# A decoder kernel whose key-mask products take 64 rows in place of six

## The chip, the cores and the metric

The kernel runs on one core of a Trainium2 chip. Its time is the device time of one execution in microseconds, taken as the median over several executions.

## What is computed

Two decoder layers on x (16 sequences of 64 tokens, 128 features), each with self attention, cross attention to a context of 64 tokens, and a feed-forward part; a layer norm follows every residual sum. Layer 0 has rotary causal self attention and a mixture of eight experts of which each token takes two; layer 1 has wide self attention (16 heads of 64) and a ternary feed-forward part. Both cross attentions are narrow (16 heads of 8 features) and have a key mask:

```python
q, k, v = split_heads(x @ Wq.T), split_heads(ctx @ Wk.T), split_heads(ctx @ Wv.T)
scores = einsum('bhqd,bhkd->bhqk', q, k) / sqrt(8)
scores = where(mask == 0, NEG, scores)      # NEG: -1e9 in layer 0, -1e12 in layer 1
out = einsum('bhqk,bhkd->bhqd', softmax(scores), v)
x = layernorm(x + out @ Wo.T)
```

(Layer 0 also has biases.) The mask is 16 x 1 x 1 x 64: one row of keys for each sequence.

## The kernel before

**Tiles.** A tile is two sequences, 128 tokens in the 128 partitions; there are eight. The program has three streams of work in order: `pre` (self0, the rotary self attention, then cross0, eight tiles each), the routed experts, and `post` (the wide self attention, then cross1, then the ternary part). self0, cross0 and cross1 are objects of one class, `Narrow`.

**Order.** Each engine runs its own loop over slots j (`stream_pe`, `stream_act`, `stream_dve`, `stream_pool`), written by hand. In slot j TensorE scores tile j-2 (`s_pe`), transposes the output of tile j-5 (`y_pe`, L582), projects queries and keys of tile j (`qk_pe`, L511) and values of tile j-2 (`v_pe`, L523), transposes the exponentials of tile j-3 (`t_pe`, L429), projects the output of tile j-5 (`o_pe`, L586), weighs the values of tile j-4 (`va_pe`, L566) and transposes a normalised tile (`x_pe`, L371). Engines are joined by semaphores; a wait stands at the start of the step that needs it.

**The scores.** For a tile, `s_pe` first makes four f32 products (L539): for each sequence b (64 query columns of the array, 64 output partitions) and each half g of the heads (64 rows of the array, one PSUM bank), queries QS against the block keys KB, 512 columns. It leaves each sum open and adds four bf16 mask products to it. In self0 (L547) the stationary operand is a 64 x 64 identity and the moving one the causal fill, 64 rows, repeated over eight heads. In the cross attentions (L550) the fill value times sqrt(8), split in three bf16 parts for each of two sequences, stands in six rows of `fills` in each half (partitions 0 to 5 and 64 to 69), and the mask of the tile's keys as 0 or 1 in the same six rows of `mrb`. The sum over the six rows adds the fill to the masked keys of the right sequence.

**What reads the scores.** The DVE takes the maximum of each head (L403) and subtracts it (L413), ScalarE makes the exponentials (L419), TensorE transposes them (L429). GpSimd (POOL) makes the block keys KB (L690), the normalisation (L331, L333, L337) and the residual with bias (L716). For a y tile the DVE makes reciprocals (L676) and ysb (L680), which `y_pe` transposes.

**The start.** POOL sets `half`, `zero` and `VB` by memsets (L1996 to L1999), waits for the constants `cst` and copies ones into `VB` (L2004). The DVE waits for the same constants, casts the identity and the causal fill to bf16 (L2031, L2032), waits for both, casts the six rows of `fills` in each half (L2035), and goes on with the first PSUM copies. TensorE waits for those fills (`s_bfc`) after its first transposes. The mask rows of `mrb` are written by the DVE in slot 2 (L1795). SP issues nearly all loads in one list, then waits for `zero` (`s_zt`), stores zeros to `routed_rows`, and loads the rest of the weights (L1945).

**The last slots of cross0** have routing work between them: in slot 16 TensorE makes the first router logits (L1364) and the DVE chooses experts from them (L1378 to L1395) before it takes the next residual; in slot 17 it turns ranks into rows (L1423 to L1430). The expert weights are transposed from L1347 on. The experts' gate products are L1549. In `post` the wide attention's last tile ends among the first tiles of cross1: L910 is its last step on POOL before the transposes of its shares.

Of the kernel before, what the change touches and what calls it, by code (L numbers as in the profile page):

```python
# [8 lines left out]
BF16 = mybir.dt.bfloat16  # L9
# [6 lines left out]
P = 128  # L16
BATCH, SEQ = 16, 64
NT = BATCH * SEQ // P
# [60 lines left out]
def decoder_kernel(nc, A, out):  # L79
    with ExitStack() as ctx:  # L80
        def sb(name, shape, dt=F32):
            return ctx.enter_context(nc.sbuf_tensor(name, shape, dt))

        def sem(name):
            return ctx.enter_context(nc.semaphore(name))
# [15 lines left out]
        def bc(ap, axis, n):  # L101

            shape = list(ap.shape)
            shape.insert(axis, n)
            return ap.unsqueeze(axis).to_broadcast(shape)
# [22 lines left out]
        bvc = sb("bvc", [P, 2])  # L128
        rowb = sb("rowb", [P, 3, P])
        mk = sb("mk", [P, NT, P])  # L130
        mrb = sb("mrb", [70, NT, SEQ], BF16)
        idb = sb("idb", [P, P], BF16)
        caus = sb("caus", [P, SEQ], BF16)
        fills = sb("fills", [70, 2, P], BF16)
        QS = sb("QS", [P, 3, P])
        TMP = sb("TMP", [P, 2, 4, SEQ])
        TC = sb("TC", [P, 2, 4, SEQ])
# [94 lines left out]
        s_mk = sem("masks_made")  # L232
        s_bf = sem("bf16_identity_made")
        s_bfc = sem("bf16_constants_made")
        s_z = sem("blocks_zeroed")
        s_tern = sem("ternary_weights_made")
        s_out = sem("output_stored")
# [214 lines left out]
        class Narrow(Stage):  # L452
# [76 lines left out]
            def s_pe(self, pe, job):  # L529
                i, n = job.i, job.n  # L530
                pe.wait_ge(*self.q_ready.at(i + 1))
                if job.before:
                    pe.wait_ge(*job.before.s_read())
                for b in range(2):
                    pe.wait_ge(*self.kb.at(2 * i + b + 1))
                    q = slice(64 * b, 64 * b + 64)
                    for g in range(2):
                        f = slice(64 * g, 64 * g + 64)
                        pe.matmul(PS[q, B_S + g, :], QS[f, n % 3, q], KB[f, n % 2, b].rearrange("p h k -> p (h k)"),  # L539
                                  start=True, stop=False)  # L540
                for b in range(2):
                    q = slice(64 * b, 64 * b + 64)
                    for g in range(2):
                        o = PS[q, B_S + g, :].rearrange("q (h k) -> q h k", h=8)
                        if self.fill is None:
                            f = slice(64 * g, 64 * g + 64)
                            m = pe.matmul(o, idb[f, f], bc(caus[f, :], 1, 8), start=False, stop=True)  # L547
                        else:
                            f = slice(64 * g, 64 * g + 6)
                            m = pe.matmul(o, fills[f, self.fill, q], bc(mrb[f, i, :], 1, 8), start=False, stop=True)  # L550
                m.then_inc(self.s_mm.sem, 1)

# [696 lines left out]
        def stream_dve(dve, tiles, extra, last):  # L1249
            for j in range(last):  # L1250
                y = at(tiles, j - 5)
                if y:
                    y.stage.y_dve(dve, y)
                t = at(tiles, j - 3)
                hidden = t and isinstance(t.stage, Ternary)
                if hidden:
                    t.stage.sum_dve(dve, t)
                ternary, others = [], []
                for x in turned(tiles, j):
                    (ternary if isinstance(x.stage, Ternary) else others).append(x)  # L1260
                for x in others:
                    x.stage.ln_dve(dve, x)
                if t and not hidden:
                    t.stage.sum_dve(dve, t)
                v = at(tiles, j - 2)
                if v:
                    v.stage.max_dve(dve, v)
                b, q = at(tiles, j), at(tiles, j - 1)
                if q:
                    q.stage.qkw_copies(dve, 1, q)  # L1270
                if v:
                    v.stage.vw_copies(dve, 1, v)
                extra(dve, j, False)
                w = at(tiles, j - 4)
                if w:
                    w.stage.ya_dve(dve, w)
                for r in summed(tiles, j):
                    r.stage.r_dve(dve, r)
                for x in ternary:
                    x.stage.ln_dve(dve, x)  # L1280
                if b:
                    b.stage.qk_dve(dve, b)
                extra(dve, j, True)

        def stream_pool(pool, tiles, extra, last):
            for j in range(last):
                t = at(tiles, j - 3)
                if t:
                    t.stage.shares_pool(pool, t)
                extra(pool, j, False)  # L1290
                b = at(tiles, j - 1)
                if b:
                    b.stage.blocks_pool(pool, b)
                b = at(tiles, j)
                if b:
                    b.stage.cos_pool(pool, b)
                if t:
                    t.stage.hidden_pool(pool, t)
                for r in summed(tiles, j):
                    r.stage.rsqrt_pool(pool, r)  # L1300
                for x in turned(tiles, j):
                    x.stage.bias_pool(pool, x)
                extra(pool, j, True)
# [574 lines left out]
        def drain_dve(dve):  # L1878
            a1.y_dve(dve, S[5])
            moe.choose(dve, 1)  # L1880
            a1.r_dve(dve, S[5])
            a1.y_dve(dve, S[6])
            a1.ln_dve(dve, S[4])
            moe.place(dve, 1)
            a1.ln_dve(dve, S[5])
            a1.r_dve(dve, S[6])
            a1.y_dve(dve, S[7])
            moe.choose(dve, 2)
            a1.ln_dve(dve, S[6])
            a1.r_dve(dve, S[7])  # L1890
            moe.place(dve, 2)
            a1.ln_dve(dve, S[7])
            moe.choose(dve, 3)
            moe.place(dve, 3)

        def drain_pool(pool):
            a1.rsqrt_pool(pool, S[5])
            moe.scatter(pool, 2, 0)
            moe.scatter(pool, 2, 1)
            a1.rsqrt_pool(pool, S[6])  # L1900
            moe.scatter(pool, 3, 0)
            moe.scatter(pool, 3, 1)
            a1.rsqrt_pool(pool, S[7])
            for t in range(4, NT):
                for r in range(2):
                    moe.scatter(pool, t, r)
# [87 lines left out]
        @block.gpsimd  # L1994
        def _(pool):
            pool.memset(half[:, :], -0.5).then_inc(s_half, 1)  # L1996

            pool.memset(zero[:, :], 0.0).then_inc(s_zt, 1)
            pool.memset(VB[:, :, :, :, :, :], 0.0).then_inc(s_z, 1)  # L1999
            pool.wait_ge(s_cst, 16)  # L2000
            pool.wait_ge(s_z, 1)
            for b in range(2):
                for a in range(2):
                    pool.tensor_copy(VB[:, :, :, b, a, DH], bc(cst[:, C_HALF + a:C_HALF + a + 1], 1, 3).to_broadcast([P, 3, PAIRS]))\  # L2004
                        .then_inc(s_z, 1)
            pool.wait_ge(s_half, 1)
            for h in range(2):
                pool.wait_ge(s_x[h], 16)
            pool.wait_ge(s_b[0], 16 * NB)
            stream_pool(pool, pre, pre_pool, len(pre) + 2)  # L2010
            drain_pool(pool)
            moe.pool(pool)
            stream_pool(pool, post, post_pool, len(post) + DEPTH)
# [13 lines left out]
        @block.vector  # L2027
        def _(dve):
            dve.wait_ge(s_id, 16)
            dve.wait_ge(s_cst, 16)  # L2030
            dve.tensor_copy(idb[:, :], ident).then_inc(s_bf, 1)  # L2031
            dve.tensor_copy(caus[:, :], cst[:, C_CAUSAL:C_CAUSAL + SEQ]).then_inc(s_bf, 1)  # L2032
            dve.wait_ge(s_bf, 2)
            for f in (slice(0, 6), slice(64, 70)):
                dve.tensor_copy(fills[f, :, :], cst[f, C_FILL0:C_FILL0 + 2 * P].rearrange("p (l q) -> p l q", l=2))\  # L2035
                   .then_inc(s_bfc, 1)
            first.copies(dve, 1)
            dve.tensor_copy(onesb[:, :], cst[:, C_ONES:C_ONES + P]).then_inc(s_rt, 1)
            dve.tensor_copy(trib[:, :], cst[:, C_BEFORE:C_BEFORE + P]).then_inc(s_rt, 1)
            dve.memset(before[:, 0, :], 0.0).then_inc(s_rt, 1)  # L2040
            stream_dve(dve, pre, pre_dve, len(pre) + 2)
            drain_dve(dve)
            moe.dve(dve)
            stream_dve(dve, post, post_dve, len(post) + DEPTH)
# [27 lines left out]
```

## Time and profile before

| | us |
|---|---|
| median of 3 runs | 376.67 |
| lowest, highest | 373.87, 377.61 |
| span of the profiled execution | 377.6 |
| TensorE busy (matmul) | 336.8 |
| VectorE (DVE) busy | 236.4 |
| GpSimd (POOL) busy | 202.1 |
| ScalarE (ACT) busy | 183.6 |

The profile is of one execution, whose span is 0.9 us above the median of the runs. PE is TensorE's matmuls and PEld its weight loads, which overlap them; ends of matmuls are modelled. One f32 matmul stands in the records as several. Times in the views are microseconds from the span's start unless marked ns; L550 is line 550 of the kernel. In the chain of work that ended last, each step is followed back to what released it; "issue" is time in which the engine waited for nothing that the profile shows. The granted clock is TensorE's, as a share of 2.4 GHz.

### The profile page before, as it was taken

To read this page: it belongs to the slowest core of one execution; us is meant where nothing else is said; L and a number is where in the kernel's file an instruction comes from. 1 tells how busy PE (TensorE), PEld (TensorE's weight loads), DVE (VectorE), ACT (ScalarE), POOL (GpSimd) and SP (SyncE) were. 2 spreads that over 40 slices of the span, in tenths; PEclk is the share of its full clock that TensorE was granted. 3 is DMA by queue.
4 is the path that set the end of the run, shared out by engine and by line. 5 is a ranking of instruction groups with operands and counts; after the bars stand their busy time and mean duration, and the time that the engine had idled before them with its cause. 6 is when DMAs were issued, how large, how long until landed. Compare 5 with 4: busy or idle time off the path is not lost.

```text
span 377.6 us, 9893 instructions
## 1 busy us (share of the span) xinstructions
PE 336.8 (89%) x3774; PEld 264.6 (70%) x3774; DVE 236.4 (63%) x561; ACT 183.6 (49%) x383; POOL 202.1 (54%) x287
## 2 busy tenths in 40 slices
PE   3879999998885589999997799889999999999994
PEld 2556677665774489999997675657788665676773
DVE  2798987778755013574335477746666577887585
ACT  2466776665653823233224134433544344776641
POOL 1856988885667124553413776322222057476785
PEclk9989999999989669999999699999999999999999
DMA  6799996000001101111101111000000000000001
GB/s 191 219 308 256 293 338 176 2 3 2 30 28 51 43 16 49 50 43 50 44 27 33 36 36 30 2 0 2 2 2 3 3 0 3 2 2 2 3 21 36
DMA packets 35993, 22.98 MB, mean 61 GB/s; under 512 B 4196, under 2 KB 33900, under 8 KB 35820
## 3 DMA queue, kind: packets, MB, share of 16 engines
q1 hardware_dynamic: 34636, 19.64, 17.9%
q0 software_dynamic: 1024, 2.10, 1.9%
q8 instruction: 31, 0.51, 0.5%
q10 hardware_dynamic: 288, 0.62, 0.5%
q14 instruction: 14, 0.11, 0.1%
HBM read 14.61 MB, written 7.73 MB: 59 GB/s over the span
## 4 chain that ended last, share of the span: by engine, by line
PE 76%; DVE 11%; issue 5%; ACT 3%; POOL 2%; DMA 1%; another core or an unknown queue 1%; SPq 0%; POOLq 0%; ACTq 0%; DVEq 0%
PE banks L429 7%; PE banks L844 7%; PE banks L831 6%; PE banks L1549 6%; PE banks L1557 6%; PE banks L539 6%; PE banks L566 6%; PE banks L1580 6%; PE banks L875 3%; PE banks L1347 3%; PE banks L511 3%; PE banks L523 2%; PE banks L1032 2%; PE banks L586 2%; PE banks L582 2%
## 5 line engine op out<-in xcount | busy, mean ns | idle before, releaser
L690 POOL TENSOR_TENSOR KB<-KT,cst 128x512 f32<-128x512 f32 x48 | 49.3, 1048 | 8.2 <-DVE KT L650 6.0
L403 DVE TENSOR_REDUCE mx<-banks 128x16 f32<-128x1024 f32 x32 | 38.6, 1207 | 13.5 <-PE banks L550 11.7
L438 ACT ACTIVATE PT<-banks 128x512 f32<-128x512 f32 x64 | 34.9, 595 | 23.6 <-PE banks L429 22.3
L1572 DVE TENSOR_TENSOR PT<-banks,PR 128x512 f32<-128x512 f32 x23 | 15.9, 691 | 47.9 <-PE banks L1557 43.7
L1537 POOL COPY U<-WALL 128x1024 f32 x21 | 21.9, 1043 | 42.6 <-PE banks L1557 35.9
L881 ACT ACTIVATE U<-banks 128x512 f32<-128x512 f32 x40 | 23.9, 597 | 38.1 <-PE banks L844 22.5
L331 POOL TENSOR_SCALAR ve<-mv 128x1 f32<-128x1 f32 x40 | 9.1, 229 | 54.0 <-DVE mv L326 53.6
L429 PE MATMUL banks<-cst,PR 128*128 128x128 f32 x256 | 35.6, 283 | 0.5 <-POOL PR L910 0.5
L419 ACT ACTIVATE PR<-PR 128x1024 f32<-128x1024 f32 x32 | 33.8, 1058 | 3.4 <-DVE PR L413 3.4
L831 PE MATMUL banks<-XT,WQKV 128*128 128x128 f32 x256 | 33.2, 292 | 0.4 <-ACT XT L1750 0.4
L844 PE MATMUL banks<-WALL,XT 128*64 128x512 f32 x128 | 29.7, 600 | 3.1 <-DVE U L881 2.8
L831 PEld LDWEIGHTS banks<-XT,WQKV 128*128 128x128 f32 x256 | 31.6, 205 | 1.1 <-ACT XT L1750 0.7
L429 PEld LDWEIGHTS banks<-cst,PR 128*128 128x128 f32 x256 | 28.3, 144 | 4.2 <-issue 2.0
L539 PE MATMUL banks<-KB,QS 64*64 64x512 f32 x192 | 27.8, 632 | 3.2 <-DVE PR L413 2.2
L413 DVE TENSOR_TENSOR PR<-banks,mx 128x1024 f32<-128x1024 f32 x24 | 29.4, 1225 | 0.8
L566 PE MATMUL banks<-VB,PT 128*64 128x18 f32 x768 | 26.7, 212 | 0.0
L566 PEld LDWEIGHTS banks<-VB,PT 128*64 128x64 f32 x768 | 24.3, 138 | 3.1 <-issue 0.3
L1549 PE MATMUL banks<-XGT,U 128*128 128x128 f32 x184 | 25.8, 286 | 0.0
L1557 PE MATMUL banks<-XGT,U 128*128 128x128 f32 x184 | 25.2, 281 | 0.0
L881 DVE COPY U<-banks 128x512 f32<-128x512 f32 x24 | 16.2, 687 | 14.2 <-PE banks L844 11.0
L1580 PE MATMUL banks<-WALL,PT 128*128 x184 | 24.4, 276 | 0.6 <-DVE YS L1588 0.6
L333 POOL TENSOR_TENSOR rstd<-ve,half 128x1 f32<-128x1 f32 x40 | 23.2, 579 | 3.3
(190 smaller groups left out, 699.5 us busy)
## 6 DMA issues: line engine op xcount, KB each, us to landing
routed_rows<-zero SPq DMA_DIRECT2D x1, 4544.0 KB, 19.1
WALL<-in_L_ffn_wg_dram SPq DMA_DIRECT2D x8, 256.0 KB, 5.0
WALL<-in_L_ffn_wu_dram SPq DMA_DIRECT2D x8, 256.0 KB, 5.3
WALL<-in_L_ffn_wd_dram SPq DMA_DIRECT2D x8, 256.0 KB, 5.7
U<-in_L_attn_W_qkv_dram SPq DMA_DIRECT2D x1, 1536.0 KB, 23.0
XG<-routed_rows SPq DMA_DIRECT2D x23, 64.0 KB, 1.8
routed_rows<-YS SPq DMA_DIRECT2D x23, 64.0 KB, 1.6
cst<-shape_constants ACTq DMA_DIRECT2D x1, 537.0 KB, 4.6
```

Source lines behind the costliest of these rows:

```text
L403: dve.tensor_reduce(mx[:, n % 2, :], s, AX.X, ALU.max).then_inc(self.max.sem, 1)
L429: t = pe.transpose(PS[:, B_PT + m, P * (r % 4):P * (r % 4 + 1)], PR[:, n % 2, P * r:P * (r + 1)], ident)
L438: act.activation(PT[:, n % 2, 4 * m:4 * m + 4, :].rearrange("p r q -> p (r q)"), PS[:, B_PT + m, :], ACT.Copy).then_inc(self.pt.sem, 1)
L539: pe.matmul(PS[q, B_S + g, :], QS[f, n % 3, q], KB[f, n % 2, b].rearrange("p h k -> p (h k)"), start=True, stop=False)
L566: m = pe.matmul(PS[64 * b:64 * b + 64, B_Y, w * r:w * (r + 1)], PT[:, n % 2, r, 64 * b:64 * b + 64], VB[:, n % 3, r, b].rearrange("p a e - ...
L690: pool.tensor_tensor(KB[:, n % 2, b], bc(KT[:, n % 2, b, :], 1, 8), bc(cst[:, C_HEAD:C_HEAD + 8], 2, SEQ), ALU.mult).then_inc(self.kb.sem, 1)
L831: m = pe.matmul(PS[:, bank, P * k:P * (k + 1)], WQKV[:, f // 2, P * u:P * (u + 1)], XT[:, P * i:P * (i + 1)], start=True, stop=True)
L844: m = pe.matmul(PS[64 * a:64 * a + 64, bank, :], XT[:, SEQ * (2 * i + b):SEQ * (2 * i + b + 1)], WVO[:, a, 4 * g:4 * g + 4, :].rearrange(" ...
L881: return eng.activation(o, s, ACT.Copy) if part == 0 else eng.tensor_copy(o, s)
L1549: m = pe.matmul(PS[:, j % 2, P * c:P * (c + 1)], WE[:, j % 3, 0, P * c:P * (c + 1)], XGT[:, j % 3, :], start=True, stop=True)
L1557: m = pe.matmul(PS[:, 2 + j % 2, P * c:P * (c + 1)], WE[:, j % 3, 1, P * c:P * (c + 1)], XGT[:, j % 3, :], start=True, stop=True)
L1580: m = pe.matmul(PS[:, 7, 0:P], HT[:, j % 2, c, :], WALL[:, e, 2, P * c:P * (c + 1)], start=(c == 0), stop=(c == CH - 1))
```

## The change

`fills` and `mrb` become 128 partitions high in place of 70, POOL sets both to zero at the start, and the DVE waits for that before it casts the six rows of each half. The mask products of the cross attentions read 64 rows of each half in place of six; 58 of them are zero in both operands. What is written into the six rows is as before. The scores' values don't change.

```diff
--- before.py
+++ after.py
@@ -128,10 +128,10 @@
         bvc = sb("bvc", [P, 2])
         rowb = sb("rowb", [P, 3, P])
         mk = sb("mk", [P, NT, P])
-        mrb = sb("mrb", [70, NT, SEQ], BF16)
+        mrb = sb("mrb", [P, NT, SEQ], BF16)
         idb = sb("idb", [P, P], BF16)
         caus = sb("caus", [P, SEQ], BF16)
-        fills = sb("fills", [70, 2, P], BF16)
+        fills = sb("fills", [P, 2, P], BF16)
         QS = sb("QS", [P, 3, P])
         TMP = sb("TMP", [P, 2, 4, SEQ])
         TC = sb("TC", [P, 2, 4, SEQ])
@@ -232,6 +232,7 @@
         s_mk = sem("masks_made")
         s_bf = sem("bf16_identity_made")
         s_bfc = sem("bf16_constants_made")
+        s_mz = sem("mask_rows_zeroed")
         s_z = sem("blocks_zeroed")
         s_tern = sem("ternary_weights_made")
         s_out = sem("output_stored")
@@ -546,7 +547,7 @@
                             f = slice(64 * g, 64 * g + 64)
                             m = pe.matmul(o, idb[f, f], bc(caus[f, :], 1, 8), start=False, stop=True)
                         else:
-                            f = slice(64 * g, 64 * g + 6)
+                            f = slice(64 * g, 64 * g + 64)
                             m = pe.matmul(o, fills[f, self.fill, q], bc(mrb[f, i, :], 1, 8), start=False, stop=True)
                 m.then_inc(self.s_mm.sem, 1)
 
@@ -1995,6 +1996,8 @@
         def _(pool):
             pool.memset(half[:, :], -0.5).then_inc(s_half, 1)
 
+            pool.memset(fills[:, :, :], 0.0).then_inc(s_mz, 1)
+            pool.memset(mrb[:, :, :], 0.0).then_inc(s_mz, 1)
             pool.memset(zero[:, :], 0.0).then_inc(s_zt, 1)
             pool.memset(VB[:, :, :, :, :, :], 0.0).then_inc(s_z, 1)
             pool.wait_ge(s_cst, 16)
@@ -2031,6 +2034,7 @@
             dve.tensor_copy(idb[:, :], ident).then_inc(s_bf, 1)
             dve.tensor_copy(caus[:, :], cst[:, C_CAUSAL:C_CAUSAL + SEQ]).then_inc(s_bf, 1)
             dve.wait_ge(s_bf, 2)
+            dve.wait_ge(s_mz, 2)
             for f in (slice(0, 6), slice(64, 70)):
                 dve.tensor_copy(fills[f, :, :], cst[f, C_FILL0:C_FILL0 + 2 * P].rearrange("p (l q) -> p l q", l=2))\
                    .then_inc(s_bfc, 1)
```

## Rows read from the trace of the kernel before

**Rows 1.** The page: the span, TensorE's granted clock in 40 slices, the chain by engine.

```profile
span 377.6 us, 9893 instructions
...
PEclk9989999999989669999999699999999999999999
...
PE 76%; DVE 11%; issue 5%; ACT 3%; POOL 2%; DMA 1%; another core or an unknown queue 1%; SPq 0%; POOLq 0%; ACTq 0%; DVEq 0%
```

**Rows 2.** The chain, 50 to 60 us: start, us, what (last tile self0, first cross0).

```profile
50.08 1.04 PE banks L566 x32
...
52.40 0.22 PE banks L547 x4
...
54.95 1.04 PE banks L566 x32
...
57.27 0.34 PE banks L550 x4
...
59.95 1.04 PE banks L566 x32
```

**Rows 3.** Timelines of PE and PEld, a self0 and a cross0 tile: start, us, engine, line, idle before.

```profile
30.72 1.09 PE L539 MATMUL banks<-KB,QS 64*64 64x512 f32 x8
31.20 0.13 PEld L547 LDWEIGHTS banks<-caus,idb 64*64 64x64 bf16 x4 [0.28 <-issue]
...
66.17 1.09 PE L539 MATMUL banks<-KB,QS 64*64 64x512 f32 x8
67.19 0.11 PEld L550 LDWEIGHTS banks<-mrb,fills 6*64 6x64 bf16 x4 [0.81 <-issue]
```

**Rows 4.** A cross0 slot: length; busy PE, PEld, DVE, ACT, POOL; clock, DMA share, GB/s.

```profile
67.20:72.20 5.00, 5.00 (x76) 3.50 (x72) 3.86 (x8) 3.50 (x8) 4.08 (x7) 1.00 0.02 3
```

**Rows 5.** The chain at cross0's seventh group, then timelines of PE and DVE at the eighth.

```profile
87.23 0.34 PE banks L550 x4
...
93.34 0.41 PE L550 MATMUL banks<-mrb,fills 6*64 6x512 bf16 x4
93.79 0.33 PE L582 MATMUL banks<-cst,ysb 128*128 128x128 f32 x1
...
93.44 0.29 DVE L680 TENSOR_TENSOR ysb<-banks,rs 128x128 f32<-128x128 f32 x1
```

**Rows 6.** Cross1: timelines of PE and POOL at its first group, the chain at the others.

```profile
308.74 0.41 PE L550 MATMUL banks<-mrb,fills 6*64 6x512 bf16 x4
...
310.61 1.90 POOL L910 TENSOR_TENSOR PR<-PR,rs 128x1024 f32<-128x1024 f32 x1 [2.57 <-DVE rs L920]
312.57 1.09 PE L429 MATMUL banks<-cst,PR 128*128 128x128 f32 x8 [0.52 <-POOL PR L910]
...
315.65 0.34 PE banks L550 x4
...
344.88 0.34 PE banks L550 x4
```

**Rows 7.** SP's timeline: two of its issues; the chain: the first use of expert weights.

```profile
29.65 1.04 SPq L1945 DMA_DIRECT2D routed_rows<-zero  x1
...
57.93 0.86 SPq L1945 DMA_DIRECT2D WALL<-in_L_ffn_wd_dram  x1
...
102.29 0.44 PE banks L1347 x4
```

**Rows 8.** POOL's timeline at the start of the program.

```profile
0.91 0.82 POOL L1999 MEMSET VB<- 128x864 f32 x1
5.86 0.65 POOL L2004 COPY VB<-cst 128x24 f32<-128x24 f32 x4 [4.12 <-DMA cst<-shape_constants]
```

**Rows 9.** Busy us in a stretch (columns as rows 4), and the chain's gate products.

```profile
131.90:138.70 6.80, 5.47 (x25) 5.23 (x26) 0.69 (x1) 2.16 (x6) 0.96 (x1) 0.50 0.07 19
...
134.13 1.73 PE banks L1549 x8
...
141.07 0.89 PE banks L1549 x8
```

## Prediction

> **What bounds the kernel now.** The page comes first: the reader is to see that the chain of work that ended last is 76% TensorE [rows 1]. So time inside TensorE's own stream counts, if no other engine is about to take over. Next the chain in order of time, for the last self-attention tile and the first cross-attention tile, whose TensorE steps are the same up to the mask products [rows 2]. The four mask products take 0.22 us of the chain where they are causal (L547) and 0.34 us where they are key masks (L550). The slot from one PV group (L566) to the next is 54.95 - 50.08 = 4.87 us in the self case and 59.95 - 54.95 = 5.00 us in the cross case; the difference, 0.13 us, is the mask product's and leaves nothing else to explain. The timeline of TensorE's weight loads says where it sits [rows 3]. The scores (L539, eight records) take 1.09 us in either tile. The causal products' first load starts at 31.20, while the scores run from 30.72 to 31.81. The key-mask products' first load starts at 67.19, after 0.81 us in which no load ran, only when the scores (66.17 to 67.26) are about out. Both have bf16 operands after f32 scores and 512 streamed columns; what differs is the shape, 64*64 against 6*64. Last comes the busy table of one slot: of 5.00 us TensorE is busy in all, POOL in 4.08, DVE in 3.86, ACT in 3.50 [rows 4]. TensorE alone sets the slot.
>
> **Part one: mask products over 64 rows.** There are 64 such products, four for each of 8 tiles in each of two cross attentions, so 16 groups. With the change stationary and moving operand have exactly the causal products' shape, so I price a group at the causal group's row: 0.34 - 0.22 = 0.12 us less. Bounds for a group: nothing gained at the lower end (the load still waits), and 0.13 us, the slot difference, at the upper. I take 0.12. Streaming 58 more rows of zeros costs no more by the same row, where all 64 rows are read.
>
> Now how many of the 16 groups lie on the path. In cross0 seven groups follow each other in a closed TensorE chain, the first at 57.27 and the last at 87.23 [rows 2, 5]. The seventh is also what the DVE waits for on its way into the routing work, so its gain is passed on. The eighth is not paid out: the product starts at 93.34 and the next TensorE step (L582) at 93.79, but that step needs ysb, which the DVE only finishes at 93.44 + 0.29 = 93.73, and only behind it does the DVE turn to the new scores [rows 5]. The DVE got there through routing arithmetic, whose start moves with the seven earlier groups and not with this one. I count 7 and a remainder of 0.04 us at most, which I drop.
>
> In cross1 the first group at 308.74 is absorbed too. TensorE is idle 0.52 us before the transposes at 312.57, waiting for POOL's product of PR (L910, 310.61 + 1.90), which belongs to the wide attention's last tile and reads nothing of this group [rows 6]. The other seven, from 315.65 to 344.88, are again in a closed TensorE chain. So 7 + 7 = 14 groups count.
>
> After the saving a slot is 4.88 us against POOL's 4.08, the busiest other engine, so 0.80 us of cover is left and no new bound appears [rows 4]. What follows the two stages (routing, experts, the ternary FFN) hangs on semaphores of the work ahead of it and moves earlier as a whole. The one thing tied to the program's start is the loading of expert weights, and SP issues the last of it at 57.93, over 40 us before the first expert weight is used at 102.29 [rows 7]. Nothing there holds the gain back.
>
> **Part two: zeroing the two tiles.** POOL gets two memsets at its start, of 256 and 512 bf16 elements a partition. The trace has no bf16 memset of that size. The nearest row is the 864-element f32 memset of VB, 0.82 us, and both are smaller [rows 8]; so together they cost between 0 and 1.64 us, and I take 0.7 by element count (768 / 864 x 0.82 = 0.73). They are hidden: POOL waits 4.12 us for the constants and starts its copy at 5.86. At worst that wait shrinks to 2.5 us. If this cover were gone the cost would be 0.7 us once. The zero tile is also wanted by SP for its routed-rows store, but SP issues that at 29.65, far after the memsets end [rows 7].
>
> **Part three: the DVE's new wait.** The DVE waits for both memsets after it cast identity and causal mask. Those casts themselves wait for the constants' DMA, the one that releases POOL at 5.86 [rows 8]. VB's memset, which now stands behind the two new ones, would end at 1.73 + 1.64 = 3.4 us even at the dear end. The wait is over before it is reached: 0. Queued behind it are the fills casts and the DVE's first PSUM copy, on which the first projection waits; each microsecond by which the wait were late would be a microsecond of the total. The tiles' bytes a partition don't change.
>
> **Sum.** 14 x 0.12 = 1.68 us. Against the profiled execution: 377.6 - 1.7 = 375.9 us. That execution sits 0.9 us above the median of the runs shown, so for the median 376.67 - 1.68 = 375.0 us.
>
> **One rule weighed.** The row on it: the causal loads begin at 31.20, 0.61 us before the scores' end, though scores and mask products use the same two 64-row halves [rows 3]. The Trainium skill, "TensorE: Matmul & The Clock Gate", section "What overlaps and what doesn't", says that a weight load overlaps running matmuls only when it is for another row group. By that rule the new 64-row loads could not start under the scores and the sum would be 0 instead of 1.68; the trace's causal rows disagree with it, for this pair of instructions at least.
>
> **The rivals.**
>
> No change: a load of mask weights can't run under the scores for a reason that the new form keeps, such as the fills tile being read in another way than the identity. For it: the key masks' weights are a slice of a two-layer tile, and so lie at another spacing than the causal ones, a plain square. Against it: the causal case has all the rest in common, the f32 scores ahead, the 64 columns loaded and a moving operand repeated over eight heads. Then 14 x 0 is saved: 376.7 us.
>
> Faster by more: TensorE works parts of this program at the lower clock. Between 131.9 and 138.7 the granted clock is 0.50, that is 1.2 GHz; eight gate products take 1.73 us there and 0.89 us at 141.07 at full clock [rows 9]. Ahead of that stretch TensorE had been busy for little. The saving brings the expert work in 0.84 us earlier, and such stretches can come out shorter. If half of this one fell away (3.4 us, of which half is lost time): 375.0 - 1.7 = 373.3 us; all of it, 371.6.
>
> Slower: the same mechanism with the other sign. The shifted gaps make one more such stretch of 6.8 us, over TensorE work in the expert or wide stages: 6.8 x (1 - 0.89/1.73) = 3.3 us lost against 1.68 gained, so 376.67 + 1.6 = 378.3 us. It decides from the point where about 3.5 us more of TensorE-bound work is done at the lower clock. Against it: the change makes TensorE's idle gaps no longer anywhere, and the row of granted clock has no low slice in either cross attention [rows 1]; there is no reason for this sign rather than the other.
>
> **How the numbers follow.** Forecast (1.3 to 1.9 us saved, clock as before) 0.62; no change 0.14; faster by the clock 0.13; slower by the clock 0.11. The prediction is 375.0 us; its own range is 374.7 to 375.5 if nothing but the edit moved. The three runs of before span 373.87 to 377.61, so a median of a few runs carries about a microsecond each way beside the mechanism. The range of 8 in 10 has to reach over most of the no-change case and half of each clock case: 372.6 to 377.4. A measurement of this kernel can tell about 1% (3.8 us) from no change; the forecast is 0.45%, inside that. Faster by over 1% needs 372.9 or less, the clock case and some luck: 0.10. Slower by over 1% needs 380.4 or more, two such stretches: 0.04. The rest, 0.86, is the same.
>
> **What would show it.** In the profile after: mask products of the shape 64*64; 0.22 us of chain for each group; the first mask load about 0.6 us ahead of the scores' end; slots of 4.88 us in cross0; TensorE's L582 near 93 us still waiting for ysb; POOL's wait for the constants down by about 0.7 us and the first score product where it was. The prediction is wrong if a group keeps 0.34 us, if a slot stays at 5.0 us with another engine's wait in it, or if the stretches at the lower clock differ by more than 3 us in all.

## The result

| | before | after |
|---|---|---|
| median, us | 372.97 (6 runs: 370.27 to 377.61) | 367.57 (6 runs: 365.97 to 368.49) |
| span of the profiled execution, us | 377.6 | 365.6 |

The ratio is 0.988, interval 0.9837 to 0.9923: 1.2% faster, some 4.5 us, where 1.68 us were forecast. Ratios leave out executions more than 1.5% above the fastest of the same kernel; medians are over all of them. 367.57 lies outside the range of 372.6 to 377.4. Of the 7.4 us between 375.0 and 367.57 the larger part is the base: in the larger samples below the median of the kernel before is 371.9 us, 4.8 us under 376.67, and the three runs behind 376.67 all lie above it.

### What the profile after shows

The chain, self0's last tile and cross0's first (start, us, what). All line numbers past the new lines are one higher, so the mask product is L551 and the causal one L548:

```profile
49.84 1.04 PE banks L567 x32
...
52.16 0.22 PE banks L548 x4
...
54.72 1.04 PE banks L567 x32
...
57.03 0.22 PE banks L551 x4
...
59.59 1.04 PE banks L567 x32
```

The key-mask group now takes what the causal group takes, 0.22 us for 0.34 [rows 2], and the cross slot is 59.59 - 54.72 = 4.87 us where it was 5.00, equal to the self slot's 4.88. The timelines of TensorE and of its weight loads say how:

```profile
60.82 1.09 PE L540 MATMUL banks<-KB,QS 64*64 64x512 f32 x8
61.30 0.13 PEld L551 LDWEIGHTS banks<-mrb,fills 64*64 64x64 bf16 x4 [0.28 <-issue]
```

The mask weights load 0.48 us after the scores begin and 0.61 us before they end. Before, the loads stood idle for 0.81 us and began at the scores' end [rows 3]. The busy table of one slot (length, PE, PEld, DVE, ACT, POOL, granted clock, DMA share, GB/s) still has TensorE busy throughout and POOL next [rows 4]:

```profile
67.20:72.20 5.00, 5.00 (x72) 3.64 (x71) 3.98 (x9) 3.53 (x9) 4.17 (x7) 1.00 0.01 3
```

The two groups that were not to count do not: in the timeline of TensorE L583 waits for ysb at cross0's eighth group [rows 5], and the transposes in the wide attention's last slot wait 0.52 us for POOL as before [rows 6].

```profile
92.69 0.33 PE L583 MATMUL banks<-cst,ysb 128*128 128x128 f32 x1 [0.17 <-DVE ysb L681]
...
301.22 1.09 PE L430 MATMUL banks<-cst,PR 128*128 128x128 f32 x8 [0.52 <-POOL PR L911]
```

POOL's timeline has the two memsets, 0.31 and 0.53 us, 0.72 us between the starts of the first and of `zero`; the wait for the constants is 3.25 us, down from 4.12 [rows 8]:

```profile
0.77 0.31 POOL L1999 MEMSET fills<- 128x256 bf16 x1
1.02 0.53 POOL L2000 MEMSET mrb<- 128x512 bf16 x1
1.49 0.21 POOL L2001 MEMSET zero<- 128x128 f32 x1
...
5.71 0.65 POOL L2007 COPY VB<-cst 128x24 f32<-128x24 f32 x4 [3.25 <-DMA cst<-shape_constants]
```

### Where the 12 us between the two profiles lie

Each landmark is a start in the chain, before and after.

| to | before | after | gained in this piece |
|---|---|---|---|
| first mask group of cross0 | 57.27 | 57.03 | 0.24 (0.12 of it the landing of the first weights) |
| seventh group | 87.23 | 86.28 | 0.71 |
| L582 behind the eighth | 93.79 | 92.69 | 0.15 |
| first gate products | 134.13 | 124.55 | 8.48 |
| first wide projections (L831) | 212.03 | 201.16 | 1.29 |
| cross1's second group | 315.65 | 304.30 | 0.48 |
| cross1's eighth group | 344.88 | 333.00 | 0.53 |
| end | 377.6 | 365.6 | 0.1 (the eighth group's own) |

The pieces that hold mask groups give 0.71 + 0.15 + 0.53 + 0.1 = 1.5 us. Nearly all the rest lies between cross0 and the wide attention, where the edit changes nothing. Most of the 8.48 us is one pause. In the timeline of TensorE the last transposes of expert weights, before, stand with gaps between them from 116.4 to 128.4 us:

```profile
118.98 0.66 PE L1347 MATMUL banks<-cst,WALL 128*128 128x128 f32 x4 [0.62 <-issue]
120.46 0.66 PE L1347 MATMUL banks<-cst,WALL 128*128 128x128 f32 x4 [0.82 <-issue]
123.33 1.12 PE L1347 MATMUL banks<-cst,WALL 128*128 128x128 f32 x4 [2.20 <-ACT WALL L1352]
```

After, the same 44 records stand in one block, as they do in every other profile of this document:

```profile
112.78 5.00 PE L1348 MATMUL banks<-cst,WALL 128*128 128x128 f32 x44
```

That is 12.0 us against 5.0. What held them up in that one execution no view shows. The granted clock in 40 slices, after:

```profile
PEclk9989999999999699999998799999999999999998
```

Before, the slices from 104 us on read 8, 9, 6, 6 [rows 1]; now there is one 6 in that region. So the next question was whether that is a thing of two single executions or of the two kernels.

### The profile page after: what moved, and what is told of

Read it like the earlier page. It is cut to its first block, busy times and chain, and to the rows that moved or that the text cites. A ratio compares the mean times of both kernels' runs of the same rounds, so it can differ in the third digit from the quotient of the medians.

```text
span 365.6 us, 9896 instructions
## 1 busy us (share of the span) xinstructions
PE 328.4 (90%) x3774; PEld 259.7 (71%) x3774; DVE 236.4 (65%) x561; ACT 182.6 (50%) x383; POOL 203.0 (56%) x289
## 4 chain that ended last, share of the span: by engine, by line
PE 71%; DVE 15%; issue 5%; POOL 3%; ACT 3%; DMA 2%; SPq 1%; POOLq 0%; ACTq 0%; DVEq 0%
PE banks L845 7%; PE banks L430 7%; PE banks L832 7%; PE banks L1550 6%; PE banks L1558 6%; PE banks L1581 6%; PE banks L540 5%; PE banks L567 5%; PE banks L876 3%; PE banks L512 2%; PE banks L524 2%; PE banks L1033 2%; DVE mx L404 2%; PE banks L583 2%; PE banks L859 2%
## 5 line engine op out<-in xcount | busy, mean ns | idle before, releaser
L430 PE MATMUL banks<-cst,PR 128*128 128x128 f32 x256 | 34.8, 279 | 0.5 <-POOL PR L911 0.5
L1550 PE MATMUL banks<-XGT,U 128*128 128x128 f32 x184 | 25.3, 282 | 0.0
L1707 POOL DMA_INDIRECT KB<-routed_rows,pos x16 | 15.9, 993 | 16.4 <-DMA routed_rows<-YS 12.3
```

The costliest lines, as they stand in the source:

```text
L430: t = pe.transpose(PS[:, B_PT + m, P * (r % 4):P * (r % 4 + 1)], PR[:, n % 2, P * r:P * (r + 1)], ident)
L1550: m = pe.matmul(PS[:, j % 2, P * c:P * (c + 1)], WE[:, j % 3, 0, P * c:P * (c + 1)], XGT[:, j % 3, :], start=True, stop=True)
```

## Experiments

All are one-core runs beside runs of the kernel before on the same chip. Each execution comes with its mean granted clock over the span, and the two go together: in 35 executions of the kernel before the nine with 0.977 took 369.35 to 369.80 us, those with 0.968 took 371.14 to 371.95, those with 0.963 took 371.96 to 372.25, and those with 0.950 or 0.951 took 376.58 to 376.98. The less clock, the longer the time, in levels. Two limits of this measure: a low stretch costs nothing where TensorE has nothing to run (in the changed kernel's profile the clock is 0.69 from 361 to 365.5 us and TensorE is idle), and the profiled execution of the kernel before took 377.6 us at 0.964, some 5 us above that level, which fits the pause shown above. I therefore count for each kernel how many executions had 0.965 or less ("low"), beside the median and the ratio.

### The kernel before against itself

No edit.

> The kernel before, unchanged, timed against itself. In the two profiles the last score group of cross0 is followed by the first gate product 40.3 us later before the change and 31.9 us later after it. If those 8.5 us are a thing of single executions (theory A), the profile here shows another length of that stretch than 40.3, nearer 32 to 36, and the ratio is 1.000 within half a per cent. If they belong to the old kernel's own timing (theory B), the stretch is 39 to 41 us again and all runs lie 4 us or more above the changed kernel's 367.6.

Ratio 1.0025 (0.9974 to 1.0077). The stretch from the eighth mask group to the first gate products is 92.14 to 128.83 = 36.7 us here against 40.6 in the first profile and 32.2 in the changed kernel's. In c1_only below, with cross0 untouched, it is 32.3. So theory A holds for most of the 8.5 us: a single profile of this kernel can be 4 to 8 us off there. But low executions are not rare: 8 of 12 here, and 17 of 35, 13 of 29 and 13 of 23 in the three samples of the kernel before. The changed kernel had none in 6. The busy table of two stretches (columns as above) shows what they are:

```profile
92.40:95.80 3.40, 3.39 (x23) 2.80 (x19) 2.58 (x3) 1.70 (x5) 2.79 (x3) 0.50 0.06 22
102.70:112.80 10.10, 10.10 (x67) 9.53 (x65) 4.51 (x26) 4.87 (x12) 5.67 (x8) 0.50 0.08 26
```

TensorE is busy in all of it at 1.2 GHz, in cross0's last slots and the transposes of expert weights between them.

### The zeroing without the shape

```diff
-                            f = slice(64 * g, 64 * g + 64)
+                            f = slice(64 * g, 64 * g + 6)
```

(on the changed kernel; memsets, wait and tall tiles stay)

> The changed kernel with its memsets, wait and taller tiles, but with six-row mask products. If the gain is the product's shape (theory A and B alike), this one is as before: mask groups 0.34 us, ratio 0.998 to 1.002. If the gain comes from the shifted start of POOL and DVE (theory C), most of the 1.2% stays: ratio about 0.989 with groups still at 0.34.

0.9991 (0.9947 to 1.0035), median 371.49, low 5 of 12; the group takes 0.34 us. The memsets and the wait cost and gain nothing beyond that interval, and 0.989 lies outside it. Theory C is out.

### One stage at a time

```diff
+                            f = slice(64 * g, 64 * g + (64 if self.fill == 0 else 6))   # c0_only
+                            f = slice(64 * g, 64 * g + (64 if self.fill == 1 else 6))   # c1_only
```

> 64 rows in cross0 alone. The direct saving is 7 groups, 0.84 us, ratio 0.998. If what goes beyond it arises in the routing stretch because that is reached 0.84 us sooner (theory B), this kernel has nearly all of the gain: 0.84 plus 2 to 3 us, ratio 0.989 to 0.992, and cross1 alone has 0.998.

> 64 rows in cross1 alone. All the routing and expert work is ahead of it, so theory B gives the direct saving and no more: 0.6 to 0.8 us, ratio 0.998. If the two stages gain alike for a reason not seen yet (theory D), ratio 0.994.

| | median, us | ratio | low |
|---|---|---|---|
| cross0 alone | 368.90 (367.02 to 369.46) | 0.9942 (0.9914 to 0.9969) | 0 of 12 |
| cross1 alone | 369.98 (368.66 to 374.03) | 0.9977 (0.9941 to 1.0014) | 4 of 12 |

Cross1 alone is what the sum says: the lowest execution is 0.69 us below the 369.35 of the kernel before. Cross0 alone takes off 2.2 us (1.2 to 3.2) by the ratio where the sum has 0.84, and its executions are narrow: the upper end is gone. Theory B forecast 2.8 to 3.8 us, more than that. Its reason, arriving sooner, is not needed: a kernel below that arrives no sooner keeps the clock as well. It is not excluded as one more cause either.

### 32 rows and 33 rows

```diff
+                            f = slice(64 * g, 64 * g + 32)   # r32
+                            f = slice(64 * g, 64 * g + 33)   # r33
```

> Mask products over 32 rows, 26 of them zero, in both cross attentions. If what costs 0.12 us is that a product of another row shape than the scores' 64 can't be loaded under them, 32 rows behave as six: groups of 0.34 us, load at the scores' end, ratio 0.998 to 1.002. If it is the small number of rows as such, part of the gain shows: groups between 0.22 and 0.34.

> The same over 33 rows, one more. By the shape theory the product now needs the array's 64-row quarter: groups 0.22 us as with 64, ratio 0.988 as the changed kernel. By the row-count theory it lies beside 32 rows.

The timelines of the weight loads, r32 first, then r33, and in the same order the scores they stand behind:

```profile
62.17 0.11 PEld L551 LDWEIGHTS banks<-mrb,fills 32*64 32x64 bf16 x4 [0.81 <-issue]
...
61.15 1.09 PE L540 MATMUL banks<-KB,QS 64*64 64x512 f32 x8
```

```profile
61.32 0.13 PEld L551 LDWEIGHTS banks<-mrb,fills 33*64 33x64 bf16 x4 [0.28 <-issue]
...
60.83 1.09 PE L540 MATMUL banks<-KB,QS 64*64 64x512 f32 x8
```

One row makes the difference. With 32 rows the load waits for the scores' end, the group takes 0.34 us, the ratio is 0.9966 (0.9918 to 1.0014) and 6 of 10 executions are low; with 33 the load goes ahead, the group takes 0.22 us, the ratio is 0.9883 (0.9827 to 0.9939) and none of 4 is low. So it is the row shape of the product against that of the scores, not the number of rows read. The Trainium skill, "TensorEngine Tiling (Array Packing)", section "Key Properties", says that changing the tiling mode drains the engine; this pair agrees, and puts 0.12 us on one change ahead of the mask group. The Trainium skill, "TensorE: Matmul & The Clock Gate", section "What overlaps and what doesn't", would forbid the early load for equal row groups; r33 and the changed kernel disagree with it.

### Which groups of cross0 hold the clock

```diff
+                            f = slice(64 * g, 64 * g + (64 if self.fill == 0 and i >= 6 else 6))   # g67
+                            f = slice(64 * g, 64 * g + (64 if self.fill == 0 and i < 6 else 6))    # g05
+                            f = slice(64 * g, 64 * g + (64 if self.fill == 0 and i == 7 else 6))   # g7
```

> 64 rows only in the last two groups of cross0, the ones around 87 and 93 us; all others six rows. Direct saving one group, 0.12 us. If the clock falls after cross0 because of what TensorE does in that place (theory E), the runs over 372 us vanish here too: median 369.5 to 370.5. If it needs the slots ahead of it (theory F), the runs are spread as before, 369.4 to 377, median 371 to 373.

> The complement: 64 rows in the first six groups of cross0, six rows in the last two and in cross1. Direct saving 6 x 0.12 = 0.72 us. Theory E: the runs stay spread, 368.6 to 376.3, median about 371. Theory F: narrow as with all eight, 367 to 369.5.

> 64 rows only in the eighth group of cross0 (around 93 us), where the next step waits for the DVE anyway: no direct saving. In the looks so far the clock fell at 93.08 and 92.98 us with that group in the old form, and with the new form did not fall near there at almost the same place of the clock's other changes. If that one group decides (theory E), the runs above 372 us become rare and the median is 369.6 to 371, granted clock mostly 0.968 or more. If it takes more of cross0's groups, the spread is the old one, about half the runs above 372.

| 64 rows in | direct saving | median, us | ratio | low |
|---|---|---|---|---|
| groups 7 and 8 | 0.12 | 368.98 | 0.9950 (0.9920 to 0.9981) | 0 of 12 |
| group 8 alone | none | 369.46 | 0.9954 (0.9921 to 0.9988) | 0 of 12 |
| groups 1 to 6 | 0.72 | 368.76 | 0.9924 (0.9890 to 0.9958) | 1 of 12 |

The eighth group alone, which saves no time where it stands, makes the kernel 0.46% faster and takes the low executions away. That is a part of the missing gain that no saved time explains. Two pairs of profiles fit it, each with the program's earlier low stretch at the same place, so that the clock's changes can be laid side by side. First g05, then the changed kernel:

```profile
24.90:28.20 3.30, 3.30 (x20) 1.39 (x14) 2.83 (x5) 1.17 (x3) 2.31 (x3) 0.50 1.14 311
...
93.08:96.49 3.41, 3.41 (x25) 2.94 (x26) 2.51 (x3) 2.17 (x6) 2.60 (x3) 0.50 0.06 22
```

```profile
24.90:28.20 3.30, 3.30 (x22) 1.49 (x16) 2.87 (x6) 1.20 (x3) 2.23 (x3) 0.50 1.14 314
...
93.08:96.49 3.41, 3.01 (x52) 2.60 (x53) 3.11 (x7) 3.14 (x7) 2.69 (x5) 1.00 0.07 22
```

In g05 TensorE had been idle 1.09 us at 90 us, then run an eighth group of six rows at 92.47, and the clock fell at 93.08. In the changed kernel the same idle time and an eighth group of 64 rows at 92.13 stand ahead of the same place, and it stayed up. The pair z_only and r33 does the same at 93.9 us: 0.50 against 1.00. Over all fourteen profiles: of the seven with an old eighth group four fall between 92.4 and 93.9 us (b_again, z_only, r32, g05; not the first profile, c1_only, nor gap below), of the seven with the new one none does.

Groups 1 to 6 alone also leave only 1 of 12 low, which speaks against theory E as the whole cause: with the old eighth group about half should be low. The count is coarse, though. g05's own profiled execution falls twice, at 93.1 and 103.3 us, for 3.4 us each, and with 0.968 does not count as low. With the line drawn at 0.969 the shares are 62 of 87 for the kernel before, 4 of 12 for groups 1 to 6, 2 of 12 each for group 8 alone, for groups 7 and 8 and for gap below, 6 of 12 for cross1 alone, and none for cross0 alone, r33 and the changed kernel. So any of these edits to cross0 makes the falls rarer, and the eighth group is one way to it, not the only one.

### Filling the idle time in the old kernel

```diff
+                if tiles is pre and j == len(pre):
+                    for _ in range(4):
+                        pe.matmul(PS[:, B_Q, 0:P], ident, ident, start=True, stop=True)
                 for x in turned(tiles, j):
```

> The kernel before, with six-row products, and four extra products of the identity with itself (128 columns each, about 0.9 us, into a free bank, read by nobody) in TensorE's 1.08 us of idle time at 91 us. If the falls of the clock after 92 us come from that idle time together with the old mask groups (theory E), filling it takes away what c0_only took away beyond its 0.84 us: median 369.5 to 370.5, hardly a run above 372. If the clock does not depend on what TensorE does there, the spread stays, median 371 to 373; if the extra products get in the way, each run is up to 0.9 us longer.

0.9947 (0.9916 to 0.9978), median 369.78 (368.44 to 371.32), low 0 of 12. In the timeline of TensorE the extra products fill the 1.08 us, the next step starts as it would have, and the mask group behind has the old form:

```profile
90.58 1.16 PE L1215 MATMUL banks<-cst 128*128 128x128 f32 x8
91.73 0.30 PE L371 MATMUL banks<-cst,X 128*128 128x128 f32 x1
...
93.04 0.41 PE L550 MATMUL banks<-mrb,fills 6*64 6x512 bf16 x4
```

Useless work in a wait makes the old kernel as much faster as the new form of group 8 does. So two edits that have nothing in common but TensorE's activity around 90 to 93 us have the same effect, and the idle time there is part of the cause. It is not all of it: this run's profiled execution still falls at 103.2 us for 3.4 us.

### Filling two more waits in the changed kernel

```diff
                 pe.wait_ge(*last.y_read())
+                for _ in range(5):
+                    pe.matmul(PS[:, B_Y, :], ident, cst[:, 0:BANK], start=True, stop=True)
```

w2 has this and also:

```diff
+                for _ in range(1):
+                    pe.matmul(PS[:, B_Y, :], ident, cst[:, 0:BANK], start=True, stop=True)
                 fc.means_pe(pe)
+                for _ in range(2):
+                    pe.matmul(PS[:, B_Y, :], ident, cst[:, 0:BANK], start=True, stop=True)
                 pe.wait_ge(*fc.bias.at(1))
```

> The changed kernel with five extra f32 products of 512 columns (about 4.3 us, into a free bank, read by nobody) in TensorE's 4.5 us wait for the experts' first rows. Theory: the low stretch at 120.4 to 127.2 us follows from that idle time; without it the first gate and up products take 0.89 us for 1.72 and 1.38, so 1.3 to 1.7 us less than the changed kernel, 366.0 to 366.4. Rival: the extra products run at full power for nothing and the experts' start slips by what they overrun, 367.6 to 368.5.

> As w1, and three more such products in the two waits before the wide attention, around 196 and 199 us. The wide stage's first 32 records take 5.99 us in the changed kernel and 3.77 us at full clock; if the fill keeps the clock up there too, 2.2 us more are saved, so 363.8 to 364.4. If only w1's part works, 366.0 to 366.4.

| | median, us | ratio to the kernel before |
|---|---|---|
| w1 | 365.31 (363.84 to 368.65, 6 runs) | 0.9828 (0.9759 to 0.9897) |
| w2 | 364.01 (363.71 to 364.88, 6 runs) | 0.9792 (0.9741 to 0.9844) |

w2 is the best version found, 3.6 us below the changed kernel's median (3.3 us by the two ratios), and the steadiest: mean granted clock 0.992 to 1.000 in all six. The busy table of the two stretches, the changed kernel first, then w2:

```profile
120.40:127.20 6.80, 3.99 (x17) 3.49 (x18) 0.00 (x0) 3.39 (x7) 0.00 (x0) 0.50 0.24 69
198.90:205.70 6.80, 4.99 (x22) 4.72 (x23) 2.38 (x7) 1.47 (x3) 5.58 (x8) 0.50 0.14 40
```

```profile
120.40:127.20 6.80, 5.49 (x34) 3.83 (x33) 0.69 (x1) 3.78 (x8) 0.77 (x1) 1.00 0.24 69
198.90:205.70 6.80, 5.63 (x100) 5.19 (x101) 3.71 (x11) 2.35 (x5) 5.59 (x7) 1.00 0.15 40
```

The first gates take 0.90 us for the 1.72 of the changed kernel, and the wide stage's first 32 records take 3.84 us where they took 5.98. w1's median is 0.7 us better than forecast, but it is not steady: its own profile fell to the lower clock from 101.5 to 108.4 us, in the routing work, though its eighth group of cross0 has the new form.

## Why the prediction was wrong

**Right.** The shape is the cause of the 0.12 us, a group costs 0.22 us after it, the load begins 0.6 us before the scores' end, the cross0 slot is 4.87 us (4.88 forecast), groups 8 of cross0 and 1 of cross1 pay nothing directly, and the memsets are hidden (0.72 us between starts for 0.7). By the pieces that hold the groups the direct gain is 1.5 us for 1.68: cross0 gave its 0.86, cross1 0.67 for 0.84.

**A small miss: the cover.** The finding that "no new bound appears" was read from a cross0 slot with 0.80 us of cover [rows 4]. Cross1's early slots are shorter, and there a bound did appear. Of cross1's six slot intervals the first and the last three gave 0.11 to 0.13 us each, the second and third 0.03 and 0.02. In the second, the scores ahead of the fourth group wait in the code for the DVE's subtraction, which gives their banks back. The timelines of DVE and TensorE there, before, then after:

```profile
323.06 1.22 DVE L413 TENSOR_TENSOR PR<-banks,mx 128x1024 f32<-128x1024 f32 x1
324.53 1.09 PE L539 MATMUL banks<-KB,QS 64*64 64x512 f32 x8
```

```profile
311.71 1.22 DVE L414 TENSOR_TENSOR PR<-banks,mx 128x1024 f32<-128x1024 f32 x1
313.03 1.09 PE L540 MATMUL banks<-KB,QS 64*64 64x512 f32 x8
```

The subtraction ended 0.25 us ahead of the scores before and 0.10 us after, and c1_only has the same 0.10. The DVE sets that slot now. Why the next one gave little too I did not settle.

**The step that failed** is the clock's term in the sum. The forecast puts it at nothing ("clock as before"), and the slower rival gives the reason: "the change makes TensorE's idle gaps no longer anywhere, and the row of granted clock has no low slice in either cross attention [rows 1]; there is no reason for this sign rather than the other". The runs show a term with one sign, and it needs no longer gap. Cross0's eighth group stands 1.3 us behind an idle time of 1.08 us and in front of the routing work, and its form has a say in how often the clock falls. About half of the executions of the old kernel, 43 of 87 in the three samples, fell to the lower clock often enough to lose 2.5 to 8 us; of the kernels with the eighth group in the new shape, none of 46 did (c0_only, g67, g7, r33 and the changed kernel). I had priced the clock as luck with two equal signs, 0.13 to 0.11; by g7, where nothing is saved directly, it is worth 1.7 us (0.4 to 2.9), about as much as the direct gain. The two together are 3.2 of the 4.5 us. The last 1.3 lie within the intervals, and no run assigns them. The prediction's own sign of being wrong came up as well: the stretches at the lower clock sum to about 27 us in the profile before (377.6 us at 0.964) and 20 after (365.6 us at 0.973), over 3 us apart.

**The range** was too narrow on the good side for that, and it stood on a base of three runs from the upper part of the old kernel's spread. The rows had hinted at both: the low slices behind cross0 were in view [rows 1], and the spread of 3.7 us in three runs was taken as noise around a level. In the larger samples the spread is mostly the number of low stretches. The slowest of the three, the profiled one, also has the pause in its expert weights. That the base was high is luck of three executions, and it makes up more of the distance to 375.0 than the clock's term does.

**The rule weighed** was rightly set aside: r33 and the changed kernel load weights under products in the same rows.

**The no-change rival** falls with r32 and r33: what differs between six rows and the causal case is the row shape and not the spacing of `fills`.

**Left open.** How the clock comes to fall where it does. Whether the old eighth group weighs on the clock through the products themselves or through the gap ahead of them: TensorE idles the same in total there, because the next step waits for ysb either way. And why the first six groups alone nearly emptied the low end: they also arrive 0.72 us sooner, and no run separates that from their form.

## What to carry to other kernels

Look at the row shape of small products that follow each other: 33 rows with zeros can be cheaper than 6 or 32, if the neighbours use 64; here it was 0.12 us a group. Where the spread between runs of one kernel is made of levels, put the granted clock of each run beside its time before pricing anything, and look for the idle time ahead of the low stretches. Filling such waits with products that nobody reads gave 2 us of median in the old kernel (one wait) and 3.6 us in the new one (three other waits). An edit that saves nothing where it stands can still change how often the clock falls.

## What the hardware showed that was not expected

- 32 rows against 33 rows in the stationary operand: a group of four products of 512 columns behind 64-row scores takes 0.34 against 0.22 us.
- In g05's profile the clock fell to 1.2 GHz at 93.08 us with TensorE idle only 1.09 us ahead of it, then busy for 1.9 us, with a mask group of six rows last; in the changed kernel's profile it did not at the same place with a group of 64 rows.
- In r32's profile the clock stayed at 0.50 for 20.4 us in which TensorE was busy 19.57 us (the busy table):

```profile
92.98:113.40 20.42, 19.57 (x167) 16.70 (x164) 9.78 (x40) 7.88 (x18) 11.04 (x15) 0.50 0.06 20
```
